# A four-layer graph network in fp32: columns spread by a turn read with step zero, and the orders of all engines rewritten

## The reference

```python
# L0, binary:  relu(adj @ (max(sign(x), 0) @ sign(w0).T))
# L1, attention
e = where(adj != 0, exp(-leaky_relu(s_left[:, None] + s_right[None, :], 0.01)), 0)
x_a = (e / (e.sum(1) + 1e-5)) @ h            # h = x @ W_sa, s_left/right = h @ a_sa halves
x_b = adj @ (x @ W_gcnb) + b_gcnb
out = sigmoid(attn_a * x_a + attn_b * x_b)   # attn_a/b = sigmoid([adj @ x, x] @ W.T + b)
# L2, mean:  A = (adj != 0);  A @ (x @ W + b) / A.sum(0)[:, None]
# L3, two GAT layers
Wh, Ws = split(x @ W)
a = softmax(Wh @ Ws.T, axis=-1) * adj
x = leaky_relu(a @ Wh + x, 0.01)
```

## Time and profile before

| | us |
|---|---|
| median of 3 runs | 504.92 |
| lowest, highest | 501.99, 504.94 |
| profiled execution | 503.84 |
| its span | 502.0 |
| busy in the span: PE, DVE, ACT, POOL | 481.2, 349.6, 243.8, 173.1 |
| mean granted TensorE clock | 0.997 |

### The profile page before, as it was taken

How to read it: one execution, slowest core, us unless ns; L and a number is a source line. 1 busy time by engine, 2 the same in 40 slices (tenths; PEclk the granted TensorE clock), 3 DMA queues, 4 the chain that set the end, 5 groups by cost and what they waited for, 6 DMA issues and landing times.

```text
span 502.0 us, 5846 instructions
## 1 busy us (share of the span) xinstructions
PE 481.2 (96%) x1973; PEld 319.1 (64%) x1973; DVE 349.6 (70%) x757; ACT 243.8 (49%) x448; POOL 173.1 (34%) x175
## 2 busy tenths in 40 slices
PE   5999999999999989999999999999999999999994
PEld 4889855545555678878545445555556645878782
DVE  4589879999963569849233952972752289699984
ACT  5766549992877353433334533442433466343200
POOL 1421242460534028934000631451240055355531
PEclk9999999999999999999999999999999999999998
DMA  8757120000453000000000000000000000000000
GB/s 300 235 170 215 40 83 0 0 0 1 125 208 119 25 1 1 0 1 1 0 1 0 0 1 1 2 0 0 0 1 0 0 1 2 1 12 21 22 31 29
DMA packets 8149, 20.70 MB, mean 41 GB/s; under 512 B 976, under 2 KB 4708, under 8 KB 8120
## 3 DMA queue, kind: packets, MB, share of 16 engines
q1 hardware_dynamic: 6840, 18.75, 11.3%
q0 software_dynamic: 464, 0.79, 0.7%
q10 hardware_dynamic: 816, 0.79, 0.5%
HBM read 18.94 MB, written 1.39 MB: 40 GB/s over the span
## 4 chain that ended last, share of the span: by engine, by line
PE 77%; DVE 11%; issue 4%; ACT 3%; POOL 3%; DMA 1%; POOLq 0%; DVEq 0%; ACTq 0%
PE psum L1445 17%; PE psum L1227 10%; PE psum L1489 9%; PE psum L1263 9%; PE psum L1323 5%; PE psum L1555 4%; PE psum L1210 4%; PE psum L1425 4%; DVE ST L991 2%; PE psum L1282 2%; PE psum L1398 2%; PE psum L1144 2%; PE psum L1526 2%; DVE ST L987 1%; PE psum L1309 1%
## 5 line engine op out<-in xcount | busy, mean ns | idle before, releaser
L1445 PE MATMUL psum<-QT,xT 128*128 128x512 f32 (+3 forms) x264 | 108.7, 543 | 0.3 <-DVE xT L1026 0.3
L412 POOL TENSOR_TENSOR es<-es,ST 128x512 f32<-128x512 f32 (+3 forms) x60 | 72.9, 1215 | 53.7 <-ACT ST L617 52.4
L604 ACT ACTIVATE ST<-psum 128x512 f32<-128x512 f32 (+3 forms) x66 | 36.1, 547 | 84.1 <-DVE rm L965 80.3
L1445 PEld LDWEIGHTS psum<-QT,xT 128*128 128x128 f32 (+1 forms) x264 | 47.7, 186 | 40.9 <-issue 34.0
L965 DVE TENSOR_TENSOR rm<-psum,rm 128x512 f32<-128x512 f32 (+3 forms) x60 | 37.4, 624 | 41.7 <-PE psum L1445 41.4
L362 POOL TENSOR_TENSOR rstd<-veps,nhalf 128x1 f32<-128x1 f32 (+1 forms) x44 | 28.9, 658 | 94.9 <-DVE veps L772 94.8
L1555 PE MATMUL psum<-Wh,ST 128*128 128x256 f32 (+3 forms) x242 | 55.7, 381 | 1.0 <-DVE vbuf L1039 1.0
L1489 PE MATMUL psum<-ST,Wh 128*128 128x512 f32 (+3 forms) x132 | 54.4, 543 | 1.6 <-DVE vbuf L1012 1.1
L1263 PE MATMUL psum<-eb,x_all 128*128 128x512 f32 (+3 forms) x132 | 52.8, 545 | 0.0
L617 ACT ACTIVATE ST<-ST 128x512 f32<-128x512 f32 (+3 forms) x66 | 37.9, 579 | 27.4 <-DVE ST L987 24.8
L1555 PEld LDWEIGHTS psum<-Wh,ST 128*128 128x128 f32 (+3 forms) x242 | 44.3, 186 | 9.9 <-DVE vbuf L1039 1.8
(11 more groups left out here) (161 smaller groups left out, 788.2 us busy)
## 6 DMA issues: line engine op xcount, KB each, us to landing
adj_rows<-in_adj_dram SPq DMA_DIRECT2D x10, 677.0 KB, 5.6
rows<-in_adj_dram SPq DMA_DIRECT2D x10, 677.0 KB, 3.9
out_dram<-xs SPq DMA_DIRECT2D x10, 128.0 KB, 1.7
x_all<-in_x_dram SPq DMA_DIRECT2D x2, 512.0 KB, 6.8
W<-in_L_gnn_W_stack_dram SPq DMA_DIRECT2D x2, 512.0 KB, 6.2
adj_rows<-in_adj_dram SPq DMA_DIRECT2D x1, 338.5 KB
rows<-in_adj_dram SPq DMA_DIRECT2D x1, 338.5 KB
w0n<-in_L_gnn_weight_dram ACTq DMA_DIRECT2D x1, 256.0 KB, 5.2
```

The costliest lines, as they stand in the source:

```text
L412: nc.gpsimd.tensor_tensor(es[0:r, g % 2, 0:w], es[0:r, g % 2, 0:w], buf(g)[0:r, j, 0:w], ALU.add)\
L1445: last = nc.tensor.matmul(psum[0:r, SB[n % 3], 0:w], xT[l][:, k, j * P:j * P + r], QT[:, k, c0:c1], start=(k == 0), stop=(k == KD - 1))
```

## The change

1. *Spread.* `across(columns, n, r)` reads one column with step zero, 128 times; TensorE turns that against the identity, and the result is the column along the free axis on all partitions. The diagonals (`dg`, `dgd`), their ScalarE work (`max_diag`, `den_diag`, the loop over L501) and semaphores go.
2. *First stage.* `dot_columns` at i == 2 instead of 1, `spread_dots` ahead of agg_a(4) into bank 0 instead of inside agg_a(2) into bank 3, `ubc` copied behind adj_evac(4), left dots from i == 4 (three in that round).
3. *Attention and mean.* `att_t` behind all row degrees; `mean_mask(3)` behind attn_sum(2); gate, high_half(0), W3T and M3 copies reordered; `h_proj(2)` and `(3)` one place earlier; `c_part` does all six banks with the high half, then all six with the low half, and waits for the low half only there.
4. *Mean.* Five `c_proj` ahead of the first turn instead of four.
5. *Turnovers.* `spread_rden`, `rdb_evac` and `scale_t` one step earlier; in the second, `add_t` and `leaky_t` at steps 1 and 2. `wh1(0)` and `q_mul(4)` go among the sums of group 2, `wh1(1)` ahead of spread_rden(2).
6. *Last stage.* Three banks (NB3) for sum_n, `den(4)` ahead of sum_n(4), and `finish_n` cut in `read_n` and `norm_n`, with steps of their own.

```diff
+    NB3 = [2, 3, 5]
     FIN4 = {1: 0, 5: 1, 8: 2}
-    FIN5 = {1: 3, 5: 4, 8: 5, 10: 6}
+    READ5 = {1: 3, 4: 4, 8: 5, 11: 6}
+    FIN5 = {2: 3, 6: 4, 10: 5}
+    READY5 = 6
...
+        def across(columns, n, r):
+
+            return columns[0:r, n:n + 1].to_broadcast([r, P])
...
-                if i == 3:
+                if i == 4:
                     act.wait_ge(ubc_ps.sem, 1)
-                    nc.scalar.activation(ubc[:, :, :], bank(3).rearrange("p (h n) -> p h n", h=2), ACT.Copy).then_inc(ubc_ready.sem, 1)
+                    nc.scalar.activation(ubc[:, :, :], bank(0).rearrange("p (h n) -> p h n", h=2), ACT.Copy).then_inc(ubc_ready.sem, 1)
...
-            for i in range(T):
-                r = kk(i)
-                act.wait_ge(dots_done.sem, i + 1)
-                if i >= 4:
-                    act.wait_ge(dg_used.sem, i - 3)
-                nc.scalar.activation(dg[0:r, i % 4, :], ident[0:r, :], ACT.Copy, scale=nsl[0:r, i:i + 1]).then_inc(dg_ready.sem, 1)
             for c, (c0, c1) in enumerate(CH):
-                act.wait_ge(dg_used.sem, -(-c1 // P))
+                act.wait_ge(left_spread.sem, c + 1)
...
-            act.wait_ge(att_in_ready.sem, 1)
-            nc.scalar.activation(att_t[:, :, :], attraw[:, :, :], ACT.Tanh, scale=0.5).then_inc(att_t_ready.sem, 1)
             while i < T:
                 row_degree(i)
                 i += 1
+            act.wait_ge(att_in_ready.sem, 1)
+            nc.scalar.activation(att_t[:, :, :], attraw[:, :, :], ACT.Tanh, scale=0.5).then_inc(att_t_ready.sem, 1)
...
             gate(0)
+            gate(1)
             m3_evac(0)
-            gate(1)
+            gate(2)
             w3T_evac(1)
+            high_half(0)
+            scale_b2(0)
             m3_evac(1)
-            for s in range(2, T + 2):
+            for s in range(3, T + 2):
...
             for i in range(T):
-                if i == 1:
+                if i == 2:
                     dot_columns()
                 finish_a(i)
-                if i == 3:
+                if i == 4:
                     dve.wait_ge(ubc_ready.sem, 1)
                     left_dot(0)
-                if i >= 3:
+                    left_dot(1)
+                if i >= 4:
                     left_dot(i - 2)
...
-            mean_mask(3)
             dve.wait_ge(den_ps.sem, 1)
...
             attn_sum(2)
+            mean_mask(3)
...
-            def turnover(g, last):
+            def turnover(g, last, add):
...
-                    if s == 1:
+                    if s == 0:
                         scale_t(g)
-                    if s == 2:
+                    if s == add:
                         add_t(g)
+                    if s == add + 1:
                         leaky_t(g)
...
-            turnover(0, T)
+            turnover(0, T, 2)
             max_reduce(2)
-            turnover(1, CROSS)
+            turnover(1, CROSS, 1)
...
             for s in range(T + 2):
                 soft_step(5, s)
+                if s in READ5:
+                    read_n(READ5[s])
                 if s in FIN5:
-                    finish_n(FIN5[s])
+                    norm_n(FIN5[s])
                 if s - 1 in FIN5:
                     finish_out(FIN5[s - 1])
...
-                for k in range(T):
-                    if i == 2 and k == CROSS:
-                        spread_dots()
...
             for i in range(T):
+                if i == 4:
+                    spread_dots()
                 agg_a(i)
...
-                    pe.wait_ge(dg_ready.sem, i + 1)
-                    last = nc.tensor.matmul(bank(6 + c % 2, i * P - c0, i * P - c0 + r), ones[0:r, :], dg[0:r, i % 4, 0:r],
-                                            start=True, stop=True)
-                    last.then_inc(dg_used.sem, 1)
+                    pe.wait_ge(dots_done.sem, i + 1)
+                    last = nc.tensor.transpose(bank(6 + c % 2, i * P - c0, i * P - c0 + r), across(nsl, i, r), ident[0:r, 0:r])
+                last.then_inc(left_spread.sem, 1)
...
             def c_part(j):
                 r = kk(j)
-                pe.wait_ge(xl_ready.sem, j + 1)
+                pe.wait_ge(xh_ready.sem, j + 1)
                 pe.wait_ge(mask_ready.sem, j + 1)
...
-                for c, (c0, c1) in enumerate(CH):
-                    for m in range(KD):
-                        for part in range(2):
+                for part in range(2):
+                    if part == 1:
+                        pe.wait_ge(xl_ready.sem, j + 1)
+                    for c, (c0, c1) in enumerate(CH):
+                        for m in range(KD):
...
             turn_w3(0)
             h_proj(1)
+            h_proj(2)
             mul_w3(0)
             turn_w3(1)
-            h_proj(2)
+            h_proj(3)
             mul_w3(1)
-            h_proj(3)
...
-                    pe.wait_ge(dgm_ready.sem, tiles_to(g) + n + 1)
-                    last = nc.tensor.matmul(bank(7, n * P, n * P + r), ones[0:r, :], dg[0:r, n, 0:r], start=True, stop=True)
+                    last = nc.tensor.transpose(bank(7, n * P, n * P + r), across(negmax, n, r), ident[0:r, 0:r])
...
                 if j0 == 0:
-                    pe.wait_ge(gat_read.sem, NC + max(i - 1, 0))
+                    pe.wait_ge(gat_read.sem, NC + max(i - 2, 0))
...
-            for i in range(4):
+            for i in range(5):
                 c_proj(i)
...
                 s_tile(2, s)
-                if s == 1:
+                if s == 0:
                     spread_rden(0)
...
+            den(4)
             for i in range(EB, CROSS):
                 sum_n(i, 0, T)
-                if i == EB:
-                    den(4)
```

More of the change, by code:

```diff
@@ L284, in tiles @@
             return range(c0 // P, -(-c1 // P))
-        def tiles_to(g):
-            return sum(len(tiles(n)) for n in range(g))
+        def across(columns, n, r):
+            return columns[0:r, n:n + 1].to_broadcast([r, P])
         @block.sync
@@ L604, in st_copy @@
                 nc.scalar.activation(buf(g)[0:r, j, 0:w], psum[0:r, SB[n % 3], 0:w], ACT.Copy).then_inc(st_ready.sem, 1)
-            def max_diag(g):
-                act.wait_ge(negmax_ready.sem, g + 1)
-                if g >= 1:
-                    act.wait_ge(max_ready.sem, g)
-                for n, i in enumerate(tiles(g)):
-                    r = kk(i)
-                    nc.scalar.activation(dg[0:r, n, :], ident[0:r, :], ACT.Copy, scale=negmax[0:r, n:n + 1]).then_inc(dgm_ready.sem, 1)
             def exp_probs(g, j):
@@ L622, in wh1_evac @@
                 nc.scalar.activation(Wh[1][0:r, i, :], psum[0:r, WB[i], 0:D], ACT.Copy).then_inc(wh1_ready.sem, 1)
-            def den_diag(g):
-                act.wait_ge(rden_ready.sem, g + 1)
-                if g >= 1:
-                    act.wait_ge(rden_spread.sem, g)
-                for n, i in enumerate(tiles(g)):
-                    r = kk(i)
-                    nc.scalar.activation(dgd[0:r, n, :], ident[0:r, :], ACT.Copy, scale=rden[0:r, g, n:n + 1]).then_inc(dgd_ready.sem, 1)
             def rdb_evac(g):
@@ L1027, in leaky_t, with read_n @@
                     .then_inc(xT1_ready.sem, 1)
-            def finish_n(i):
+            def read_n(i):
                 r, g = kk(i), NC + (i * P) // BANK
@@ L1108, in _ @@
                 if s in FIN4:
-                    finish_n(FIN4[s])
+                    read_n(FIN4[s])
+                    norm_n(FIN4[s])
                 if s - 1 in FIN4:
@@ L1113, in _ @@
                 soft_step(5, s)
+                if s in READ5:
+                    read_n(READ5[s])
                 if s in FIN5:
-                    finish_n(FIN5[s])
+                    norm_n(FIN5[s])
                 if s - 1 in FIN5:
                     finish_out(FIN5[s - 1])
-            first = len(FIN4) + len(FIN5)
-            for i in range(first, T):
-                finish_n(i)
-                if i > first:
-                    finish_out(i - 1)
+            norm_n(READY5)
+            for i in range(len(FIN4) + len(READ5), T):
+                read_n(i)
+                norm_n(i)
+                finish_out(i - 1)
             finish_out(T - 1)
@@ L1190, in spread_dots @@
                 pe.wait_ge(ub_ready.sem, 2 * KD)
-                pe.wait_ge(adjT_banks_read.sem, 3 * BANKS_T + 1)
+                pe.wait_ge(adjT_banks_read.sem, 4 * BANKS_T + 1)
                 for half in range(2):
                     for k in range(KD):
-                        last = nc.tensor.matmul(bank(3, half * D + k * P, half * D + (k + 1) * P), Ub[:, half, k, :],
+                        last = nc.tensor.matmul(bank(0, half * D + k * P, half * D + (k + 1) * P), Ub[:, half, k, :],
                                                 ident[:, :], start=True, stop=True)
@@ L1325, in c_part @@
                                                     stop=(j == T - 1 and part == 1))
-                        if j == T - 1:
-                            last.then_inc(c_done.sem, 1)
```

(21 more changed lines are left out.)

45 lines of the change are left out of this document (18 added, 27 removed).

## The result

The changed kernel took 491.6 us (median of 4 runs, 489.76 to 491.76) beside 504.74 for the kernel before (4 runs, 501.99 to 504.94): a ratio of 0.9744, 95% interval 0.9703 to 0.9784. The forecast was 491.7. The profiled execution took 491.76 us, 1.86 more than its span.

The account below looks back on a forecast made before the run. TensorE, busy 481.2 of 502.0 us, was taken as the bound, so only fewer passes and waits help. Passes 5.0 plus the stages' waits summed to 12.1 off 503.84, giving 491.7 us, range 488.5 to 497.5.

Parts of the forecast that it names:

- mean stage: From the c_projs on: a fifth c_proj covers VectorE's first norm, against a new 0.4 us wait on cT; 0.5 us less.
- third group: Sums of group 2: wh1(0) fills the wait for masked tile 7, wh1(1) covers den(2)'s reciprocals; 0.9 us less.
- Passes: All 44 column spreads: one turn of 0.109 us each instead of two passes of 0.222 us together; 5.0 us less.
- slow turns: Rival on the spreads: turns take 0.286 us apiece with no overlap, giving 499.5 us; chance 0.05.
- First stage: Later dot_columns and spread_dots only move the waits, as VectorE is nearly packed; 0, range 0.5 us either way.
- Left scores: Left-score spread: waits for the diagonals go, only 0.35 us for the first nslb copy remains; 1.1 us less.
- Attention to mean: Reordered stage up to c_part: hT and h_proj(0) start earlier, c_part stops waiting for the low half; 1.7 us less.
- c_part's order: c_part's 11 tiles: more bank changes might cost 2.5 us, or avoiding consecutive passes on one bank save 2.5; taken as 0.
- First turnover: Before the first scale_t: diagonals gone and spread, copy and scale_t one step earlier remove TensorE's wait; 1.1 us less.
- Second turnover: At leaky_t(1): earlier scale_t, add_t and leaky_t shorten TensorE's 0.3 us wait; 0.3 us less, range 0 to 0.5.
- Last stage: sum_n(6) and sum_n(7): three banks and earlier reads remove waits for VectorE to read tiles 4 and 5; 1.5 us less.
- Waits only move: Rival across the kernel: the passes go but waits come back elsewhere, giving 497.8 us; chance 0.12.

## Why the prediction was right

The likeliest case came true: 12.1 us forecast, 11.9 measured without the two effects at the start and in the middle, and none of the rivals. That the median came within 0.1 us of the number is luck: the forecast stands on an execution with a slow start, and three of the four measured ones, among them the profiled one with its fall, have a mean clock of 0.993. Two steps, too (mean stage, third group), were off by 0.7 in opposite directions. By its steps:

- **Passes, -5.0.** Right. Four turns with step zero stand in 0.44 us:

```profile
304.35 0.60 PE L1455 MATMUL psum<-ident,negmax 128*128 128x128 f32 x4
304.79 1.88 PE L1468 MATMUL psum<-ST,Wh 74*128 74x512 f32 x4
```

0.110 a turn, 44 records instead of 88, and 272 ns for one record by itself, as the adjacency's 286 in the earlier trace rows. The slow turns (0.286 apiece) and the slow load (0.444) are both excluded: the step of zero costs nothing. The figure of the Trainium skill that I set against it ("TensorE: Matmul & The Clock Gate", Part 4: PE-mode transpose, about 275 ns, for bf16) agrees here with the length of one record, and not with the pace in a row, 0.110.
- **First stage, 0.** +0.24, within the 0.5 given, and the wait came where the step put it: agg_a(4) was to start at 35.1 on the scale of before, and 33.08 + 1.99 = 35.07; agg_a(6) at 43.15, and 41.10 + 1.99 = 43.09. What was wrong is the other side of the comparison: in the timeline of before they start at 35.20 and 42.87, and not at 35.45 and 43.12. Those are the chain's rows, which begin where the piece ahead ends, modelled end included.
- **Left scores, -1.1.** With the 22 passes 2.3 was due (11 x 0.113 + 1.1), 2.27 measured; 0.3 of wait on nslb left where I had said 0.35.
- **Attention to mean, -1.7.** 1.6, by undoing it, and by 72.10 against 73.72 from h_part(0) to c_part(0). One reason in it was wrong: that TensorE starts on the high half. That gave 0.11; the wait of 1.1 is gone without it, most likely because high_half(0) moved ahead on ScalarE, though no run moves it alone. The 0.25 of "2.74 against 2.48" was no time either: 2.74 contains the modelled end of the last matmul, and c_part(0) to c_part(1) takes 3.25 before and 3.24 after.
- **c_part's order, 0 between -2.5 and +2.5.** About -0.2 for all 11 tiles, 2.46 instead of 2.49 a tile. Neither explanation that I had bounded it by holds: bank changes cost nothing, and two passes in a row on one bank almost nothing. What a tile holds beyond 2.25 stays open.
- **Mean stage, -0.5.** It lost 0.2: -0.17 from c_proj on, and +0.35 ahead of it, where c_proj(0) waits for cT. The term that failed is what I left out: wh_mean(4)'s wait on bank 5, 0.42 (17.32 against 16.90). The wait on cT, priced at 0.4, cost 0.46, and the cover by the fifth c_proj gave 17.49 - 16.80 = 0.7 where 0.9 was due. I had followed who waits for VectorE, not which bank two neighbours share once a c_proj no longer stands between them.
- **First turnover, -1.1.** With 8 turns (0.9) 2.0 was due, 2.07 measured.
- **Second turnover, -0.3, and third group, -0.9.** Both lie behind sum_t(2, 0). With 7 turns (0.8) 2.0 was due, 2.64 measured: too small by 0.65. The trace of before shows three places:

```profile
358.64 3.49 PE L1489 MATMUL psum<-ST,Wh 128*128 128x330 f32 x12
362.44 1.98 PE L1445 MATMUL psum<-QT,xT 128*128 128x512 f32 x4 [0.30 <-DVE xT L1026]
...
372.74 1.27 PE L1489 MATMUL psum<-ST,Wh 128*128 128x330 f32 x4
374.50 4.75 PE L1489 MATMUL psum<-ST,Wh 128*128 128x330 f32 x16 [0.49 <-DVE ST L991]
...
383.10 1.03 PE L1526 MATMUL psum<-W,xT 128*128 128x256 f32 x4
384.24 1.03 PE L1512 MATMUL psum<-dgd,ones 128*128 128x128 f32 x6
```

From start to start 3.80 for twelve passes that take 3.34 after (351.39 to 354.73): 0.46 for a listed wait of 0.30. Four passes take 1.76 where 1.11 is their time in the neighbouring groups: 0.65 for a listed 0.49. And wh1(0) takes 1.14 to the spread where 0.86 is its own time: 0.3 of waiting for the diagonals that no row lists, as it is not much longer than the modelled end of the matmul ahead; with the turns alone, where the diagonals are gone and the orders kept, it takes 0.86 (377.44 to 378.30). Listed waits were too small a base. The reason that I gave for adding 0.1 to 0.2 to each, a pipeline that fills anew, is not shown: both waits cost 0.16 more than listed, and 0.16 is also what the modelled end of a row of four passes reaches past the next start (1.27 long, 1.11 to the next).
- **Last stage, -1.5.** With 7 turns (0.8) 2.3 was due, 2.30 measured, and it hangs on the third bank.

Of the signs that I had named one came out otherwise: TensorE is busy 473.1 us, where 476 was given. I did not follow that up.

*Waits only move* was the rival that mattered. Undoing the orders shows how near it was: the turns alone gave 0.8 of 6.1 back to waits, and their 497.6 us is what that rival had forecast (497.8). It fell because the orders were there too.

## What to carry to other kernels

When TensorE is busy for 96% of the span, take passes out and reorder in one go: the passes alone bring TensorE to its next wait earlier, and a part of them is lost there. When an instruction is pulled ahead out of a row, look at its two former neighbours: which bank or buffer do they share, and who has to read it between them. A short wait can be in no list, since it hides in the modelled end of the matmul ahead; the distance from start to start, held against the same instructions elsewhere, shows it. For the same reason take starts from a timeline and not from the chain. And cut both traces at the same instructions before comparing totals: here 1.99 us at the start and 1.7 us of low clock in the middle nearly cancelled in the sum. Where a stretch changes, look on both sides of its border: a wait that stands just ahead of the cut is booked to the stage before.
